# Operator stage of a graph network kernel: the bias by matrix-vector steps between the blocks of the powers, edge weights by an indirect load, node degrees in the main part, one wait for each input at the head

## The chip, the cores and the metric

The kernel runs on one core of one Trainium2 chip. Its time is the device time of one execution in microseconds, as the median of several runs. The core has TensorE (PE, matmuls), VectorE (DVE), ScalarE (ACT), GpSimd (POOL) and SyncE (SP, which issues most loads and stores); each works through its own list of instructions in order, and semaphores tie them together.

## What is computed

Four layers of graph networks over x (16 x 512 x 128), each added to x and normalised. What matters here is the first one and what the later ones need from the adjacency and the edge list:

```python
def _L0_gnn_ref(x, adj_mx, alpha_train, w, d, fc_in_w, fc_in_b, vt):
    x0 = x
    h = jnp.einsum('bnd,ed->bne', x, fc_in_w) + fc_in_b
    alph = jax.nn.sigmoid(alpha_train)[:, None]
    w_eff = w * jnp.clip(d, 0.0, 1.0) @ w.T
    dt = 1 / 8
    for _ in range(8):
        ax = jnp.einsum('nm,bmd->bnd', adj_mx, h)
        h = h + dt * (alph * 0.5 * (ax - h) + h @ w_eff - h + x0)
    return h
# layer 2: deg = row sums + column sums - diagonal of (A + I); dinv = rsqrt(deg)
# layer 3: e = e + jnp.log(A0[src, dst] + EPS)[None, :, None]     (256 edges)
```

The eight steps are linear in h, so the kernel writes their result as a polynomial in L (512 x 512: a scaled adjacency with its diagonal) and R (128 x 128, from w_eff): it needs the first, second and third power of L, eight powers of R, nine matrices E of 128 x 128, and one bias over nodes and features that stands for fc_in_b.

## The kernel before

`phase_operators` (lines 85 to 550) makes these operators once, `phase_main` (from 632) runs layers 1 and 2, then come `phase_batchnorm` and `phase_attention`. Each phase is a block that all engines leave together, so the main part starts when the last engine of the operator stage is done. TensorE works on 8 banks of PSUM in the hand-written `order` (lines 162 to 164): `begin(name, needs)` (424) waits until VectorE has emptied the tile seven places back and those it needs, `done` reports the tile. A power of L is built in four tiles (`L2T0` to `L2T3`, `L3T0` to `L3T3`; `l_power`, 448), each of 4 x 3 matmuls of 128x128 by 128x512 (`product`, lines 63 to 67: high by high, high by low, low by high; so the records stand at lines 65 to 67). ScalarE copies each tile's high part (244) and VectorE subtracts for the low part (`split` and `low_part`, line 72).

At the head (lines 184 to 232) SP loads w, the whole adjacency A in one piece, the edge lists and then x; ScalarE's queue loads alpha, d, the bias and fc_in_w, and its sigmoid (232) waits for the first three of them. VectorE makes L from A in four row blocks (279, 281), ScalarE rounds each (236), VectorE takes the low parts (285), and TensorE transposes L when all of it is there (438 to 443).

The bias goes by Horner's rule: U holds (0, 1, row sums of L) and is multiplied by L once (`UT`, 476); V holds combinations of the powers of R with the bias (498); `B2` and `B01T` (504, 510) multiply the two, and two steps `T` and `S` with the third power of L (`bias_horner`, 457) follow behind the last power, each turned back by four transposes (468).

The edge weights A[src, dst] are found with matmuls: sorted one-hot rows `Gs` of the sources are multiplied with all of A (`ROWS0`, `ROWS1`, 538), masked with the targets' `Gd` (411) and summed (`LG`, 548); ScalarE takes the logarithm (251). The sorting permutation (`perm`, 336) gives the sorted ends (`PERM`, 529; `SMALL`, 522), which SP writes to memory (197). The degrees come from row sums (355), column sums on TensorE (517), and the diagonal (357, 359); GpSimd takes the root (220), and `DROW` (544) makes a row of them that SP writes out (200).

VectorE also builds the matrices E: 9 starts (347) and 36 updates (369) from the powers of R. In the main part the prologue (`prologue`, line 821) mixes set-up tiles (`set_tiles`: transposes of A and the LSTM weights) with the first samples; `row_sum_diagonal`, at line 1614, scales the identity by the row sums.

## Time and profile before

| what | us |
|---|---|
| median of three runs (1060.51 to 1065.15) | 1063.21 |
| the profiled execution | 1063.46 |
| its span in the profile | 1061.5 |
| PE busy | 947.9 (89%) |
| DVE busy | 678.0 (64%) |
| ACT busy | 540.3 (51%) |
| POOL busy | 300.6 (28%) |

The profile is one execution. Times are counted from the start of its span. A row of a time line names the start, the duration, the engine and line, the operation, the tile written and the tiles read, shapes, and how many like instructions were merged into it; in brackets stands the idle time before it and who ended it. Matmuls overlap, so the distance between starts says more of their cost than the duration. An fp32 matmul leaves two records, one with fp32r operands one.

### The profile page before, as it was taken

The page shows a single profiled execution, that of the slowest core. Times are in us where ns is not written, and L with a number is a line of the kernel's source. Part 1 is how long each engine was busy: PE and PEld are TensorE (multiplying, and loading weights), DVE is VectorE, ACT ScalarE, POOL GpSimd, SP SyncE. Part 2 cuts the span into 40 slices and gives each one's busy share as a digit, 9 for nine tenths or more (in the row PEclk, how much of TensorE's full clock was granted, in tenths as well). Part 3 has the DMA queues.
Part 4 walks back from the last instruction along what each step waited for, and adds up shares of the span by engine and source line. Part 5 has one row for each costly group of instructions (what it writes and reads, how often), then busy time and mean ns, then how long its engine had stood idle before and what let it go on. Part 6 is the DMA issues. An engine that isn't in the chain of part 4 may idle for free. (4 is left out here: it accounts for less than half of the span.)

```text
span 1061.5 us, 14487 instructions
## 1 busy us (share of the span) xinstructions
PE 947.9 (89%) x5168; PEld 810.5 (76%) x5168; DVE 678.0 (64%) x1653; ACT 540.3 (51%) x1114; POOL 300.6 (28%) x279
## 2 busy tenths in 40 slices
PE   3989998889998999999899999989989987768984
PEld 2677997778998788899788998878778974355763
DVE  4843434434565744775674675568887875779897
ACT  2023233365554555564555545356667747466644
POOL 0001121223231312333222332232342230045643
PEclk9989999999999999999999999999999998889987
DMA  8003001000101010001001010301010000000014
GB/s 213 1 1 78 21 40 60 21 20 1 41 1 41 1 40 20 6 35 41 1 2 39 20 41 1 106 12 40 21 41 20 2 0 1 1 1 1 1 40 119
DMA packets 33881, 31.61 MB, mean 30 GB/s; under 512 B 8338, under 2 KB 27922, under 8 KB 33812
## 3 DMA queue, kind: packets, MB, share of 16 engines
q1 hardware_dynamic: 32852, 30.64, 9.3%
q8 instruction: 41, 0.67, 0.3%
q14 instruction: 28, 0.23, 0.1%
q10 hardware_dynamic: 960, 0.07, 0.1%
HBM read 22.83 MB, written 7.87 MB: 29 GB/s over the span
## 5 line engine op out<-in xcount | busy, mean ns | idle before, releaser
L1306 ACT ACTIVATE gates<-psum,gbias 128x256 f32<-128x256 f32 (+2 forms) x312 | 158.2, 565 | 56.5 <-PE psum L67 52.8
L65 PE MATMUL psum<-LS,WI 128*128 128x256 f32 (+2 forms) x312 | 105.5, 338 | 14.0 <-ACT gates L1306 10.2
L72 POOL TENSOR_TENSOR LS<-A,LS 128x512 fp32r<-128x512 f32 (+2 forms) x44 | 48.8, 1109 | 202.1 <-ACT LS L1291 202.1
L66 PE MATMUL psum<-LS,WI 128*128 128x256 f32 (+2 forms) x312 | 104.2, 334 | 0.0
L67 PE MATMUL psum<-LS,WI 128*128 128x256 f32 (+2 forms) x312 | 104.2, 334 | 0.0
L72 POOL TENSOR_TENSOR LS<-Hodd,LS 128x512 fp32r<-128x512 f32 (+2 forms) x44 | 48.6, 1106 | 160.2 <-ACT LS L1291 160.2
L65 PEld LDWEIGHTS psum<-LS,WI 128*128 128x128 f32 x312 | 60.4, 194 | 25.6 <-POOL LS L72 10.3
L72 DVE TENSOR_TENSOR yl<-psum,yh 128x512 fp32r<-128x512 f32 x58 | 39.7, 689 | 57.2 <-ACT yh L1248 41.4
L65 PE MATMUL psum<-B2h,LT2h 128*128 128x256 f32 x256 | 72.8, 284 | 1.1 <-DVE X L1414 1.0
L1313 ACT ACTIVATE tc<-cell 128x512 f32<-128x512 f32 (+2 forms) x88 | 45.2, 514 | 55.7 <-DVE cell L1594 39.9
L67 PE MATMUL psum<-B2h,LT2l 128*128 128x256 f32 x256 | 72.4, 283 | 0.0
L66 PE MATMUL psum<-B2l,LT2h 128*128 128x256 f32 x256 | 72.4, 283 | 0.0
L65 PE MATMUL psum<-Eh,yh 128*128 128x384 f32 x168 | 58.5, 348 | 12.0 <-DVE yl L72 12.0
L66 PEld LDWEIGHTS psum<-LS,WI 128*128 128x128 f32 x312 | 60.5, 194 | 5.1
L67 PEld LDWEIGHTS psum<-LS,WI 128*128 128x128 f32 x312 | 60.6, 194 | 4.2
L72 POOL TENSOR_TENSOR XSl<-X,XSh 128x512 fp32r<-128x512 f32 x32 | 42.4, 1329 | 69.0 <-ACT XSh L1243 68.7
L65 PE MATMUL psum<-LS,WH 128*128 128x256 f32 (+2 forms) x192 | 60.1, 313 | 0.0
L66 PE MATMUL psum<-LS,WH 128*128 128x256 f32 (+2 forms) x192 | 59.8, 312 | 0.0
L67 PE MATMUL psum<-LS,WH 128*128 128x256 f32 (+2 forms) x192 | 59.8, 312 | 0.0
L67 PE MATMUL psum<-Eh,yl 128*128 128x384 f32 x168 | 57.7, 344 | 0.0
L66 PE MATMUL psum<-El,yh 128*128 128x384 f32 x168 | 57.6, 343 | 0.0
L566 DVE BATCH_NORM_STATS2 nstats<-X 128x6 f32<-128x128 f32 x256 | 54.1, 277 | 0.4
(387 smaller groups left out, 2714.6 us busy)
## 6 DMA issues: line engine op xcount, KB each, us to landing
WI<-lstm_weights SPq DMA_DIRECT2D x14, 512.0 KB, 3.5
WH<-lstm_weights SPq DMA_DIRECT2D x11, 512.0 KB, 4.5
X<-in_x SPq DMA_DIRECT2D x16, 256.0 KB, 4.8
out<-X SPq DMA_DIRECT2D x16, 256.0 KB, 2.3
lstm_weights<-WI SPq DMA_DIRECT2D x4, 512.0 KB, 2.6
lstm_weights<-WH SPq DMA_DIRECT2D x3, 512.0 KB, 2.6
A<-in_adj SPq DMA_DIRECT2D x1, 1024.0 KB, 5.9
z_A<-in_adj SPq DMA_DIRECT2D x1, 1024.0 KB, 5.4
```

Source lines behind the costliest of these rows:

```text
L65: pe.matmul(out, lhs[0], rhs[0], start=start, stop=False)
L66: pe.matmul(out, lhs[0], rhs[1], start=False, stop=False)
L67: return pe.matmul(out, lhs[1], rhs[0], start=False, stop=stop)
L72: return eng.tensor_tensor(out, full, high.bitcast(F32), ALU.subtract)
L566: return dve.bn_stats(self.stats[:, bass.ds(self.sh.C * n + c, 1), :], self.sh.X[:, c, bass.ds(n, 1), :])
L1306: act.activation(gates[:, gate, 0:n], sh.psum[:, gate, 0:n], ACT.Tanh if gate == G else ACT.Sigmoid, bias=gbias[:, p_ - 1, gate:gate + 1]) ...
L1313: act.activation(tcs[:, 0:n], cell[:, s % 2, 0:n], ACT.Tanh).then_inc(S["tanh_done"], 1)
```

## The change

The bias is built from matrix-vector steps. Four groups `UA` to `UD` hold pairs of vectors (ones, and L applied to them again and again) in high and low parts, 4 columns in all; `UA` multiplies by L, `UB` to `UD` by the second power, each in 8 wide matmuls that stand between the blocks of the powers. After each of the first three, four transposes (`TA`, `TB`, `TC`) bring the vectors back, and VectorE adds high and low and splits again. `BIAS` multiplies the four groups by V in 16 small products at the very end. The Horner steps, `B2`, `B01T` and `UT` are gone.

The edge weights are loaded by GpSimd with two indirect loads of 128 elements each, at addresses that VectorE computes from src and dst; they are spread to 16 columns and multiplied by the permutation (`LG`). The row gathering with A and its masks are gone, and `PERM` and `SMALL` stand earlier.

Column sums, diagonal, root and the row of the degrees move to the main part's prologue: the column sums come from VectorE over the transposed tiles of A, the row is one more set-up tile `deg`, and its write stands in SP's list there.

At the head A comes in four pieces with a semaphore each, alpha, d and the bias have one each, the broadcast edge lists are loaded behind the first four pieces of x; the transposes go row block by row block; the low parts of L go to GpSimd; the first block of the second power waits piece by piece. wTd is made after L. VectorE's 36 updates of E are cut into pieces between its other work, and ScalarE's copy of E comes after `L3T2` instead of `L2T3`.

```diff
-        order = ["wT", "R", *(f"LT{j}" for j in range(C)), "R2", "UT", "L2T0", "R34", "L2T1", "R58", "L2T2", "FR03",
-                 "L2T3", "FR47", "FR8V", "L3T0", "B2", "L3T1", "B01T0", "B01T1", "L3T2", "L3T3", "SMALL", "T", "PERM", "T'",
-                 "ROWS0", "ROWS1", "S", "DROW", "S'", "LG"]
+        a_in = [sem(f"a_in_{c}") for c in range(C)]
+
+
+        order = ["wT", *(f"LT{j}" for j in range(C)), "R", "L2T0", "R2", "L2T1", "UA", "R34", "L2T2", "R58", "L2T3",
+                 "PERM", "SMALL", "TA", "FR03", "FR47", "FR8", "UB", "L3T0", "TB", "V", "UC", "L3T1", "TC", "LG", "UD",
+                 "L3T2", "L3T3", "BIAS"]
         at = {n: i for i, n in enumerate(order)}
-        his = [n for n in order if n[:2] in ("LT", "L2", "L3", "B2", "T'")]
+        his = [n for n in order if n[:2] in ("LT", "L2", "L3") and n != "LG"]
...
+        def rows_of(j):
+
+            if j == 0:
+                return 0, (2,)
+            if j == 1:
+                return 0, (0,)
+            g, r = divmod(j - 1, 2)
+            return g, (r, r + 2)
...
-            sp.dma_start(sh.A[:, :, :], d["adj"].rearrange("(c p) m -> p c m", p=P)).then_inc(S["a_in"], 16)
+            for c in range(C):
+                sp.dma_start(sh.A[:, c, :], d["adj"][c * P:(c + 1) * P, :]).then_inc(a_in[c], 16)
...
+                if q == 0:
+                    for k, name in enumerate(("src", "dst")):
+                        sp.dma_start(ir[:, k, :], d[f"L3_gnn_{name}"].rearrange("(o e) -> o e", o=1)
+                                     .broadcast_to([P, NE])).then_inc(S["ir_in"], 16)
...
-            sp.wait_ge(S["dve_tile"], at["DROW"] + 1)
-            sp.dma_start(sh.degrees, drow[0:1, :]).then_inc(S["ss_done"], 16)
-            sp.wait_ge(S["ss_done"], 32)
+            sp.wait_ge(S["ss_done"], 16)
...
+            for c in range(C):
+                pool.wait_ge(S["lh_done"], c + 1)
+                low_part(pool, Ll[:, c, :], L[:, c, :], Lh[:, c, :]).then_inc(S["ll_done"], 1)
+            for k, value in enumerate(sh.const_values):
+                pool.memset(sh.const[:, k, :], value).then_inc(S["memsets"], 1)
+            pool.wait_ge(S["at_done"], 1)
+            table = d["adj"].rearrange("s (t o) -> (s t) o", o=1)
+            for k in range(K):
+                pool.indirect_dma_start(weight[:, k:k + 1], None, table,
+                                        bass.IndirectOffsetOnAxis(at_edge[:, k:k + 1], 0)).then_inc(S["weight_in"], 16)
+            pool.wait_ge(S["weight_in"], 16 * K)
...
-            act.wait_ge(S["small_in"], 48)
+            act.wait_ge(S["al_in"], 16)
...
-                if name == f"L2T{C - 1}":
+                if name == "L3T2":
...
-            act.wait_ge(S["pe_tile"], at["LG"] + 1)
+            act.wait_ge(S["dve_tile"], at["LG"] + 1)
...
+            def vectors_split():
+
+                link(dve.tensor_copy(U[:, :, 0:2], pair[:, :, :]))
+                low_part(dve, U[:, :, 2:4], pair[:, :, :], U[:, :, 0:2]).then_inc(S["u_done"], 1)
+
+            def vectors_out(g):
+                copy(f"U{groups[g]}", UT[:, g, :], bank(f"U{groups[g]}")[0:W, :])
+
+            def vectors_turned(g):
+                name = f"T{groups[g]}"
+                tile(name)
+                ins = dve.tensor_copy(turned[:, :, :], bank(name)[:, 0:C * W].rearrange("p (c r) -> p c r", r=W))
+                ins.then_inc(S["dve_tile"], 1)
+                dve.wait_ge(S["dve_tile"], at[name] + 1)
+                if g == 0:
+                    dve.tensor_copy(pair[:, :, 0:1], turned[:, :, 0:1])
+                    link(dve.tensor_tensor(pair[:, :, 1:2], turned[:, :, 1:2], turned[:, :, 3:4], ALU.add))
+                else:
+                    link(dve.tensor_tensor(pair[:, :, :], turned[:, :, 0:2], turned[:, :, 2:4], ALU.add))
+                vectors_split()
...
+            dve.wait_ge(S["dc_in"], 16)
+            link(dve.tensor_scalar(dclip[:, :], dcol[:, :], 0.0, 1.0, ALU.max, ALU.min))
+            dve.tensor_scalar(wTd[:, :], wT[:, :], dclip[:, 0:1], DT, ALU.mult, ALU.mult)\
+                .then_inc(S["dve_tile"], 1)
+            row_sums(0, 2)
+            copy("R", RP[:, 1, :], bank("R")[:, 0:D])
+            link(row_sums(2, C))
+            link(dve.tensor_tensor(pair[:, :, 1], sh.rs[:, :], kappa[:, :], ALU.mult))
+            dve.wait_ge(S["memsets"], 5)
+            link(dve.tensor_tensor(pair[:, :, 1], pair[:, :, 1], ldiag[:, :], ALU.add))
+            vectors_split()
+            split("L2T0")
+            dve.wait_ge(S["ic_in"], 32)
+            link(dve.tensor_copy(icf[:, :, :], icol[:, :, :]))
+            link(dve.scalar_tensor_tensor(at_edgef[:, :], icf[:, 0, :], float(N), icf[:, 1, :], ALU.mult, ALU.add))
+            dve.tensor_copy(at_edge[:, :], at_edgef[:, :]).then_inc(S["at_done"], 1)
+            dve.wait_ge(S["ir_in"], 32)
+            split("L2T1")
+            tile("UA")
+            dve.tensor_scalar(UT[:, 0, :], bank("UA")[0:W, :], sh.ident[0:W, 2:3], None, ALU.add)\
+                .then_inc(S["dve_tile"], 1)
+            copy("R34", RP[:, 3:5, :], bank("R34")[:, 0:2 * D].rearrange("p (k d) -> p k d", d=D))
+            split("L2T2")
+            copy("R58", RP[:, 5:9, :], bank("R58").rearrange("p (k d) -> p k d", d=D))
+            dve.wait_ge(S["bc_in"], 16)
+            for j in range(NCO):
+                for r in rows_of(j)[1]:
+                    ins = dve.tensor_scalar(bsel[:, j, r:r + 1], bcol[:, 0:1], binom(N_STEPS, j), None, ALU.mult)
+            ins.then_inc(S["bsel_done"], 1)
+            split("L2T3")
+            copy("PERM", ss[:, :, :], bank("PERM").rearrange("p (j e) -> p j e", j=2))
+            copy("SMALL", sh.sc[:, :], bank("SMALL")[:, 0:K])
+            vectors_turned(0)
...
+            start_e("FR03", 0, 4)
+            start_e("FR47", 4, 4)
+            start_e("FR8", 8, 1)
+            vectors_out(1)
+            vectors_turned(1)
+            copy("V", V[:, :, :], bank("V")[0:W, :].rearrange("p (g d) -> p g d", d=D))
+            dve.wait_ge(S["weight_in"], 16 * K)
+            for k in range(K):
+                ins = dve.tensor_scalar(weightb[:, k, :], ones[:, 0:R], weight[:, k:k + 1], None, ALU.mult)
+            ins.then_inc(S["spread_done"], 1)
+            dve.wait_ge(S["dve_tile"], at["FR8"] + 1)
+            link(forcing(0))
+            vectors_out(2)
+            split("L3T1")
+            vectors_turned(2)
+            copy("LG", weights[:, :], bank("LG")[0:R, 0:NE])
+            for i in (1, 2, 3):
+                link(forcing(i))
+            vectors_out(3)
+            for i in (4, 5, 6):
+                link(forcing(i))
+            forcing(7).then_inc(S["e_done"], 1)
+            split("L3T2")
...
+            copy("BIAS", sh.bias0[:, :, :], bank("BIAS").rearrange("p (c d) -> p c d", d=D))
...
+                begin(f"L{r}T{j}", [] if r == 2 else [f"L{r - 1}T{C - 1}"])
+                    if r == 2 and j == 0:
+                        pe.wait_ge(S["ll_done"], k + 1)
+                        pe.wait_ge(S["dve_tile"], at[f"LT{k}"] + 1)
...
+            def vectors(g):
+
+                name = f"U{groups[g]}"
+                begin(name, [] if g == 0 else [f"L2T{C - 1}"])
+                pe.wait_ge(S["u_done"], g + 1)
+                high, low = sh.LT[0 if g == 0 else 1]
+                for k in range(C):
+                    pe.matmul(bank(name)[0:W, :], U[:, k, :], high[:, k, :], start=(k == 0), stop=False)
+                for k in range(C):
+                    ins = pe.matmul(bank(name)[0:2, :], U[:, k, 0:2], low[:, k, :], start=False, stop=(k == C - 1))
+                done(ins)
+            def turn(g):
+                name = f"T{groups[g]}"
+                begin(name, [f"U{groups[g]}"])
                 for c in range(C):
...
+            l_power(2, 0)
+            r_power("R2", 1, 1, "R")
+            l_power(2, 1)
+            vectors(0)
+            r_power("R34", 2, 2, "R2")
+            l_power(2, 2)
+            r_power("R58", 4, 4, "R34")
+            l_power(2, 3)
+            begin("PERM")
+            begin("SMALL")
+            for q in range(K):
+                for k in range(K):
+                    ins = pe.matmul(bank("SMALL")[:, q:q + 1], perm[:, k, q * P:(q + 1) * P], icf[:, 0, k:k + 1],
+                                    start=(k == 0), stop=(k == K - 1))
+            done(ins)
+            turn(0)
+            pe.wait_ge(S["fc_in"], 16)
+            forced("FR03", 0, 4)
+            forced("FR47", 4, 4)
+            forced("FR8", 8, 1)
+            vectors(1)
+            l_power(3, 0)
+            turn(1)
+            begin("V")
+            pe.wait_ge(S["bsel_done"], 1)
+            sizes = {}
+            for j in range(NCO):
+                sizes.setdefault(rows_of(j)[0], []).append(j)
+            for g, members in sizes.items():
+                for j in members:
+                    ins = pe.matmul(bank("V")[0:W, g * D:(g + 1) * D], bsel[:, j, :], RP[:, N_STEPS - j, :],
+                                    start=(j == members[0]), stop=(j == members[-1]))
+            done(ins)
+            vectors(2)
+            l_power(3, 1)
+            turn(2)
+            begin("LG")
+            pe.wait_ge(S["spread_done"], 1)
+            for k in range(K):
+                ins = pe.matmul(bank("LG")[0:R, 0:NE], weightb[:, k, :], perm[:, k, :], start=(k == 0),
+                                stop=(k == K - 1))
+            done(ins)
+            vectors(3)
+            l_power(3, 2)
+            l_power(3, 3)
+            begin("BIAS", ["UD", "V"])
+                cols = slice(c * P, (c + 1) * P)
+                for g in range(NG):
+                    ins = pe.matmul(bank("BIAS")[:, cols], UT[:, g, cols], V[:, g, :], start=(g == 0),
+                                    stop=(g == NG - 1))
...
-        set_tiles = [("A", j) for j in range(C)] + [("rs", 0), ("WI", 2), ("WI", 3), ("WH", 1), ("WH", 2), ("WI", 0),
+        set_tiles = [("A", j) for j in range(C)] + [("rs", 0), ("WI", 2), ("WI", 3), ("WH", 1), ("WH", 2), ("deg", 0), ("WI", 0),
                                                     ("WI", 1), ("WH", 0)]
...
+                     [next(late)], [("own", 2)], giant("t", 0, 0), taps(0, 3), [("own", 3)],
...
+                if kind == "deg":
+                    sp.wait_ge(S["set_free"], n + 1)
+                    sp.dma_start(sh.degrees, degree_row).then_inc(S["deg_out"], 16)
...
+                elif kind == "deg":
+                    dve.wait_ge(S["set_mm"], n + 1)
+                    dve.tensor_copy(degree_row, bank_like(n, "A")[0:1, :]).then_inc(S["set_free"], 1)
                 else:
-                    dve.wait_ge(S["set_hi"], n + 1 - (n > C))
+                    dve.wait_ge(S["set_hi"], turned_before(n) + 1)
+                    if kind == "A":
+                        dve.reduce_sum(cs[:, j:j + 1], bank_like(n, kind), AX.X)
...
+                if q == 0 and k == 0:
+                    dve.wait_ge(S["deg_out"], 16)
...
+            def degrees():
+                dve.wait_ge(S["set_mm"], FIRST_SUMS + 1)
+                for c in range(C):
+                    ins = dve.tensor_tensor(diag[:, c, :], sh.A[:, c, c * P:(c + 1) * P], sh.ident[:, :], ALU.mult)
+                link(ins)
+                dve.tensor_tensor(deg[:, :], rs[:, :], cs[:, :], ALU.add)
+                link(dve.reduce_sum(dsum[:, :], diag, AX.X))
+                dve.scalar_tensor_tensor(deg[:, :], deg[:, :], 1.0, dsum[:, :], ALU.add, ALU.subtract)\
+                    .then_inc(S["deg_done"], 1)
+
+            def root_diagonal():
+                dve.wait_ge(S["dinv_done"], 1)
+                for c in range(C):
+                    ins = dve.tensor_scalar(diag[:, c, :], sh.ident[:, :], sh.dinv[:, c:c + 1], None, ALU.mult)
+                ins.then_inc(S["roots_done"], 1)
...
+            def degree_roots():
+                pool.wait_ge(S["deg_done"], 1)
+                pool.tensor_tensor(sh.dinv[:, :], deg[:, :], sh.const[:, sh.ROOT, 0:C], ALU.pow)\
+                    .then_inc(S["dinv_done"], 1)
...
```

## Rows read from the trace of the kernel before

**Rows 1.** The page, busy time: engine, us, share of the span, instructions.
```profile
PE 947.9 (89%) x5168; PEld 810.5 (76%) x5168; DVE 678.0 (64%) x1653; ACT 540.3 (51%) x1114; POOL 300.6 (28%) x279
```
**Rows 2.** Windows of the operator stage: stretch, its length, each engine's busy time, clock, DMA.
```profile
26.18:59.95 33.77, 32.83 (x138) 23.92 (x137) 26.81 (x93) 5.50 (x9) 0.00 (x0) 0.95 0.00 1
59.95:89.36 29.41, 25.93 (x124) 20.91 (x122) 10.87 (x26) 2.97 (x5) 1.02 (x1) 0.88 0.00 1
89.36:130.00 40.64, 40.64 (x235) 36.94 (x236) 18.07 (x44) 14.24 (x37) 7.74 (x6) 1.00 0.28 65
...
53.20:56.30 3.10, 3.10 (x8) 2.38 (x8) 1.63 (x7) 1.33 (x2) 0.00 (x0) 0.50 0.00 0
...
64.00:70.00 6.00, 6.00 (x18) 4.95 (x18) 0.23 (x2) 0.00 (x0) 1.02 (x1) 0.50 0.00 0
```
**Rows 3.** Time line at the end of the stage, VectorE, ScalarE and TensorE.
```profile
86.80 0.68 DVE L297 COPY bias<-psum 128x512 f32<-128x512 f32 x1
88.60 0.46 ACT L251 ACTIVATE lg<-psum,tiny 16x256 f32<-16x256 f32 x1 [13.99 <-PE psum L548]
...
89.36 0.63 PE L1047 MATMUL psum<-ident,X 128*128 128x128 f32 x4 [0.80 <-PEq L99]
```
**Rows 4.** DMA issues of the head: tile, issuing queue, size, us to landing.
```profile
A<-in_adj SPq DMA_DIRECT2D x1, 1024.0 KB, 5.9
...
alpha<-in_L_gnn_alpha_train ACTq DMA_DIRECT2D x1, 2.0 KB, 2.4
...
bcol<-in_L_gnn_fc_in_b ACTq DMA_DIRECT2D x1, 0.5 KB, 7.1
```
**Rows 5.** Time line of the head: ScalarE (first two, last), VectorE.
```profile
2.76 1.28 ACT L232 ACT_TABLE_LOAD   x1 [2.76 <-issue]
8.88 0.20 ACT L232 ACTIVATE gate<-alpha 128x4 f32<-128x4 f32 x1 [4.84 <-DMA bcol<-in_L_gnn_fc_in_b]
...
10.11 0.48 DVE L279 TENSOR_SCALAR L<-A,kappa 128x512 f32<-128x512 f32 x1
...
13.25 2.49 DVE L72 TENSOR_TENSOR Ll<-L,Lh 128x512 fp32r<-128x512 f32 x4
...
29.18 0.60 ACT L244 ACTIVATE LT1h<-psum 128x512 fp32r<-128x512 f32 x1 [11.48 <-PE psum L67]
```
**Rows 6.** GpSimd's time line at 110 us, and line 1614's durations, min/median/max in ns.
```profile
110.47 1.29 POOL L1699 TENSOR_TENSOR X<-X,bias 128x512 f32<-128x512 f32 x1 [4.82 <-DVE X L1414]
...
L1614 DVE TENSOR_SCALAR cell<-ident,rs x4: 164/274/1314, 110.4 to 112.0; 128x128 f32<-128x128 f32 x4
```
**Rows 7.** Time line of TensorE: transposes, first of UT's twelve, first of L2T0's, R34.
```profile
13.39 3.68 PE L441 MATMUL psum<-ident,L 128*128 128x128 f32 x16 [2.34 <-DVE L L281]
...
21.38 0.59 PE L65 MATMUL psum<-LT0h,Uh 128*3 128x512 f32 x1 [3.88 <-DVE LT0l L72]
...
26.18 0.39 PE L65 MATMUL psum<-LT0h,Lh 128*128 128x512 f32 x1
...
28.98 0.59 PE L446 MATMUL psum<-RP 128*128 128x256 f32 x2
```
**Rows 8.** Time line of TensorE: the small and the fp32 products.
```profile
46.73 1.15 PE L504 MATMUL psum<-V,UT 3*128 3x128 f32 x8 [0.94 <-DVE V L363]
...
50.79 1.98 PE L510 MATMUL psum<-UT,V 3*128 3x512 f32 x4
...
59.95 3.66 PE L517 MATMUL psum<-ones,A 128*128 128x1 f32 x32
...
85.13 1.02 PE L544 MATMUL psum<-dblock,ones 128*128 128x512 f32 x2
86.08 0.66 PE L468 MATMUL psum<-ident,bt 128*128 128x128 f32 x4
```
**Rows 9.** Time line of VectorE: the 36 updates of E, and E's low part.
```profile
46.71 8.22 DVE L369 SCALAR_TENSOR_TENSOR Ef<-RP,Ef 128x128 f32<-128x128 f32 x36
...
57.26 1.35 DVE L72 TENSOR_TENSOR El<-Ef,Eh 128x1152 fp32r<-128x1152 f32 x1
```

More of the change, by code:

```diff
@@ new lines, in row_sums @@
+            def row_sums(c0, c1):
+                for c in range(c0, c1):
+                    ins = dve.reduce_sum(sh.rs[:, c:c + 1], sh.A[:, c, :], AX.X)
+                return ins
+            dve.wait_ge(S["idn"], 1)
+            dve.tensor_copy(RP[:, 0, :], sh.ident[:, :])
+            tile("wT")
+            link(dve.tensor_copy(wT[:, :], bank("wT")[:, 0:D]))
+            dve.wait_ge(S["gate_done"], 1)
+            link(dve.tensor_scalar(kappa[:, :], gate[:, :], 0.5 * DT, None, ALU.mult))
@@ L527, in _ @@
+            begin("R", ["wT"])
+            done(pe.matmul(bank("R")[:, 0:D], wTd[:, :], wT[:, :], start=True, stop=True))
+            l_power(2, 0)
[7 more added lines that the diff above has]
+            begin("PERM")
+            pe.wait_ge(S["perm_done"], 1)
             for j in (0, 1):
@@ L542, in _ @@
-            begin("DROW")
-            pe.wait_ge(S["diag_done"], 1)
-            done(pe.matmul(bank("DROW"), ones[:, :], dblock[:, :, :], start=True, stop=True))
-            turned("S", 1)
-            begin("LG", ["ROWS1"])
+            begin("SMALL")
[3 more added lines that the diff above has]
+                                    start=(k == 0), stop=(k == K - 1))
@@ L690, in phase_main @@
         rs = sh.rs
+        degree_row = cell[0:1, 1, :]
         norm = sh.norm
```

308 lines of the change are left out of this document (68 added, 240 removed).

## The prediction

> **What bounds the kernel now.** I read the page first: PE is busy 89% of the span [rows 1], so time can be won only where PE waits or where its work is taken away. Then I looked at the stretches around the changed code. The operator stage runs from 0 to 89.36 us, where the first instruction of the main part starts; every block ends in a barrier, so the question is when that instruction can start [rows 2, 3]. The stage has three pieces. Up to 26.18 the head waits for inputs: PE is mostly idle, and when it works, UT's twelve 512-column matmuls take 4.80 us, 21.38 to 26.18, of which the last two already went at the later 0.23: the other ten stood (4.80-0.47)/10 = 0.43 apart [rows 7] (the clock column reads 1.00 here [rows 2]; the spacing tells the half pace). From 26.18 to 59.95 PE is full with the powers of L. From 59.95 to 89.36, 29.4 us, PE does sums over the adjacency, two Horner steps for the bias, and the edge one-hots. That tail is serial and partly at half clock (0.50 in 64 to 70) [rows 2]. Every microsecond taken off this stage moves all of the rest, since nothing later waits for an input that starts early: the loads are out by 26 us [rows 2].
>
> **The head.** ScalarE's gate waits for alpha, dcol and bcol together: alpha lands at 0.73+2.4 = 3.1, bcol at 1.79+7.1 = 8.9, and the gate runs at 8.88 [rows 4, 5]. With its own semaphore the gate waits only for the table load, 2.76+1.28 = 4.04. VectorE then has kappa and ldiag by about 5.0. A's four pieces replace one load that landed at 1.18+5.9 = 7.1 [rows 4]; I take the last piece at 7.1 to 7.5 and the earlier ones about 1 us apart. Scaling one block of rows costs (13.25-10.11)/4 = 0.79 us [rows 5], so without a collision all L stands at 8.2, against 13.3 before.
>
> There is a collision. The low parts of L go from VectorE (four in 2.49) to GpSimd, which takes 1.29 us for a 128x512 operation of two inputs [rows 6], and the first starts at about 6.5 while VectorE is still scaling. The trace has this pair once: during a GpSimd addition of the same shape, 1.29 us (110.47), one of VectorE's four scalings grew from 0.27 to 1.31 us [rows 6]. That is one holding the other off, not sharing. The Trainium skill (SBUF — State Buffer, "SBUF: two separate sides") says that the two engines take a common port pair as an exclusive lock, held for the whole instruction, when VectorE reads two SBUF inputs or is in a two-port mode; by it L's last two blocks each wait for one GpSimd operation, as that row does. I take two such waits, 2.6 us (bounds 0 and three waits, 3.9), on the path: L at 10.8. Behind that the last four of sixteen transposes take 0.9 at half pace (3.68/4) [rows 7], ending at 11.7, but VectorE has more to do: dclip and wTd 0.5, half a wait more on wTd 0.6, two row sums and the first split at 0.62 each, 1.9 [rows 5]. The first L-square block starts at 13.8, not at 26.18.
>
> **PE's work from there.** That block is 12 matmuls at half pace: 12 x 0.43 = 5.1 us, to 18.9. The vector step UT, 12 matmuls between 21.38 and 26.18 and 4.8 us long at half pace, is gone from in front of it [rows 7]. All that follows in PE's order, at full clock: seven more blocks of 26.18 to 28.98 = 2.80: 19.6 [rows 7]; four vector steps of 8 wide matmuls at 2.80/12 = 0.233: 7.5 (they weigh as much with 4 stationary columns as with 128, since UT's 12, with 3 columns, also took the 0.43 of the half pace); three turns of four transposes, 0.6 each by L468 (0.66 with its tail): 1.8; fp32 products: three of 512 columns at 0.95 (L544 at 85.13, the next product at 86.08), one of 256 at 0.4, two of 128 at 0.3: 3.9; V, nine products of 128 columns at the 0.23 of L517's sixteen small ones (3.66), 2.1; SMALL, four of them, 0.9; PERM, four of 256 columns at half of 0.95, 1.9; LG, two of these, 0.9; and BIAS, 16 products with 4 rows: L504 has four with 3 rows in 1.15, so 16 x 0.29 = 4.6 [rows 8]
>
> Sum 43.2, to 62.1. Of the old tail (29.4) the column sums, two Horner steps, eight transposes, the gathering of rows and the degree row are gone.
>
> **Waits in that order.** PE needs VectorE's answers, so I ran VectorE's list beside it. Its largest load, the 36 Ef updates in 8.22 us [rows 9], is now cut into pieces behind the vector steps. PE's one wait comes out at UD: after L3T1 come ScalarE's copy (0.6 [rows 5]), the split (0.6) and the turned sum and split (0.8), 2.2 us in all, of which TC and LG cover 1.4: 0.8. PERM's mask is ready some 0.3 us before PE wants it. If the splits were each 0.5 us later, UB, UC and UD would wait 1.5 us more together. At the end VectorE has the Ef updates done 4 us ahead of BIAS's end; then ScalarE's Eh, the 1.35 of El, and a split [rows 9] fit under BIAS with 1 us over. ScalarE's table load and the logarithm (0.46) also lie under BIAS, where before they ended the stage at 89.06 [rows 3].
>
> The indirect load: indices are ready at about 21, VectorE asks for the weights at about 44. No row shows such a load. The nearest are strided loads of 4-byte elements, 2.4 to 7.1 us from issue to landing (alpha, bcol) [rows 4]; two in series end by 26 to 36, so within these bounds the cost is nothing, covered by PE's blocks; uncovered it is theirs whole, rival (c). Edge rows are written out to memory earlier than before, no one waits for them. SP's queue: three more A issues put X's loads a microsecond or two later, still over 30 us ahead of need; the broadcast index rows sit behind X's first four pieces (about 13 us, wanted at 19).
>
> **Clock.** The clock fell to 0.50 at 53.2, right after PE had spent 2 us on products with three rows (L510 at 50.79), and again at 64, after L517's 3.5 us of one-column products [rows 2, 8]. BIAS is 4.6 us of four-row products followed by 1 us of copy and barrier. I expect a fall inside BIAS or right after. Half clock for half of BIAS would cost 2.3; I take 1.0, since the fall may come behind it (0 to 3.5). And 3 to 5 us of half clock at the start of the main part, where PE is busy without a gap [rows 2], cost 1.6 (0 to 2.6).
>
> Stage end: 62.1 + 0.8 + 1.0 = 63.9; copy of the bias 0.7 and barrier 0.3 (before: the copy from 86.80, ScalarE to 89.06, PE at 89.36) [rows 3]: 64.9. Saved: 24.5.
>
> **The main part** takes what is moved there. PE: one product like L544, 0.95. VectorE: four column sums (2.5), the degree chain (2.0), the root diagonal (0.9), a one-row copy (0.7): 6.1 us on an engine that is busy 18.07 of 40.64 us there, with PE waiting for it seldom; 0.5 (0 to 3). GpSimd's root (1.0) and its wait for the degrees stand before a split of x that is asked for much later; if it isn't, 1 us. SP's degree write stands between the weight spills; the first cell step waits for it, some 40 us later. With the clock's 1.6: 3.1 lost.
>
> Net: 24.5 - 3.1 = 21.4. The profiled execution is 1063.46 us (span 1061.5), within 0.3 of the median of the three runs; 1063.46 - 21.4 = 1042.1, rounded to 1042.
>
> **Rivals.** (a) No collision and no fall of the clock: 3.2, 1.0 and 1.6 less, 1036, down to 1032 if BIAS runs faster. For it: the port row is one case, and the operations may interleave well. (b) VectorE becomes the bound of the stage: each of the four vector steps has a chain PE, copy, turn, sum, split, PE, and each link in it takes 0.6 or more; three steps late by 2 us, Ef late by 2 and the 3 of the main part give +8 to +14: 1050 to 1056. Against it: VectorE was idle a good part of 26 to 60 (26.8 of 33.8 busy, with 4.8 of that moved away) [rows 2]. (c) Slower than before: the indirect load. VectorE waits for the weights in front of Ef, so in the last third of the stage everything queues behind them. The first 23 us after the indices are hidden; each further one is paid whole. From 23+22 = 45 us the gain is gone, at 50 the kernel is 5 us slower, 1069. Nothing in the trace comes near, but no such load is in it. (d) The finer waits and the order don't shorten anything, since some wait that I have not seen (a bank of the ring, a semaphore count) holds PE to the old pace: about 1060 to 1066.
>
> **Chances.** Forecast, 1034 to 1049: 0.72. (a) below 1034: 0.10. (b), 1049 to 1058: 0.13. (d) 0.02, (c) 0.03. The range, from 8 us below the forecast to 7 above, takes in the collision's and the clock's bounds and the small stalls: 1034 to 1049. About 0.5% (5 us) is what a measurement of this kernel tells from no change: faster 0.95, same 0.02, slower 0.03.
>
> **What would show it.** The first main transposes (L1047 of before) at 62 to 67 us; the gate at about 4; L's last scaling at 10 to 12 with one VectorE row over 1 us beside a GpSimd subtraction; the first L-square block at 12 to 15; PE without a wait over 1 us from there to BIAS; clock 0.50 around the change of stage; the weights landed before 36. The forecast is wrong if PE waits for VectorE in several places between the blocks, if BIAS's products cost much more than 0.29, or if the main part grows by more than 5 us.

## The result and the profile after

The changed kernel takes 1038.02 us in the median of four runs (1037.67 to 1042.06), the kernel before 1063.51 in the same comparison: ratio 0.9774, interval 0.975 to 0.9797. Forecast were 1042, with 1034 to 1049 as the range. The profiled execution took 1037.67 us, its span is 1035.6; against 1061.5 before that is 25.9 us less. First, from the page of the changed kernel, the span, the busy time of the engines and the new queue of the indirect loads.

```profile
span 1035.6 us, 14415 instructions
PE 932.7 (90%) x5120; PEld 798.0 (77%) x5120; DVE 676.9 (65%) x1662; ACT 540.0 (52%) x1112; POOL 308.2 (30%) x284
...
q0 software_dynamic: 64, 0.00, 0.0%
```

PE's busy time fell by 15.2 us [rows 1], 10.7 us less than the span: the rest is waiting that went away. The time lines of the changed kernel at the turn from the operator stage to the main part, PE, then VectorE (columns as in the rows of before):

```profile
56.31 3.83 PE L530 MATMUL psum<-V,UT 4*128 4x128 f32 x32
61.19 1.02 PE L1045 MATMUL psum<-ident,X 128*128 128x128 f32 x4 [1.05 <-PEq L99]
```
```profile
57.15 1.36 DVE L72 TENSOR_TENSOR El<-Ef,Eh 128x1152 fp32r<-128x1152 f32 x1 [0.63 <-ACT Eh L247]
58.43 0.68 DVE L72 TENSOR_TENSOR LT2l<-psum,LT2h 128x512 fp32r<-128x512 f32 x1
60.18 0.69 DVE L273 COPY bias<-psum 128x512 f32<-128x512 f32 x1 [1.07 <-PE psum L530]
```

The first main transpose runs at 61.19, before at 89.36 [rows 3]: the stage is 28.2 us shorter. The main part is 2.3 us longer (1035.6-61.19 = 974.4 against 1061.5-89.36 = 972.1). 28.2 less 2.3 is the 25.9. The 2.3 comes from one pair of profiles and is less sure than the 28.2: in three runs below with the main part of the kernel before, the span behind the first main transpose is 967.0 to 972.4 us long, and in six with that of the changed kernel, again begun at half clock, 970.9 to 974.8. The second fence shows El and the last split done at 59.1, under BIAS, which ends at 60.14. VectorE then waits 1.07 us for BIAS: PE sets the end of the stage, with one microsecond to spare.

VectorE's time line over the head of the changed kernel, and GpSimd's beside it:

```profile
4.86 0.49 DVE L310 TENSOR_SCALAR L<-A,kappa 128x512 f32<-128x512 f32 x1
5.38 0.35 DVE L312 SCALAR_TENSOR_TENSOR L<-ident,ldiag,L 128x128 f32<-128x128 f32 x1
...
6.56 1.47 DVE L310 TENSOR_SCALAR L<-A,kappa 128x512 f32<-128x512 f32 x1
8.07 1.23 DVE L312 SCALAR_TENSOR_TENSOR L<-ident,ldiag,L 128x128 f32<-128x128 f32 x1
...
10.18 1.21 DVE L316 TENSOR_SCALAR wTd<-wT,dclip 128x128 f32<-128x128 f32 x1
```
```profile
6.48 2.67 POOL L72 TENSOR_TENSOR Ll<-L,Lh 128x512 fp32r<-128x512 f32 x2 [4.30 <-ACT Lh L240]
10.04 2.50 POOL L72 TENSOR_TENSOR Ll<-L,Lh 128x512 fp32r<-128x512 f32 x2 [0.89 <-ACT Lh L240]
```

Three of VectorE's rows are 0.9 to 1.0 us longer than their twins: 1.47 against 0.49, 1.23 against 0.35, and wTd with 1.21 against the 0.29 of the kernel before. Each lies beside one of GpSimd's subtractions, and L is done at 10.08.

PE's time line in the changed kernel at the first block of the second power (13.33), the first product behind it (17.82), the vector step UA, a turn, and UD:

```profile
13.33 0.76 PE L65 MATMUL psum<-LT0h,Lh 128*128 128x512 f32 x1 [1.08 <-DVE LT0l L72]
...
17.82 0.38 PE L425 MATMUL psum<-RP 128*128 128x128 f32 x2
...
20.84 1.09 PE L446 MATMUL psum<-LT0h,U 128*4 128x512 f32 x4
...
46.50 0.41 PE L455 MATMUL psum<-ident,UT 4*128 4x4 f32 x4
...
48.76 1.09 PE L446 MATMUL psum<-LT1h,U 128*4 128x512 f32 x4 [0.89 <-DVE U L72]
```

Between 17 us and the barrier at 61 only the last of these has a wait, at UD: 0.89 us.

PE in windows of the changed kernel around the turn (stretch, its length, PE busy with instructions, granted clock, share of the DMA engines, GB/s), and the transposes of A in the main part:

```profile
58.00:60.00 2.00, 2.00 (x20) 1.00 0.00 0
60.00:62.00 2.00, 0.95 (x6) 0.82 0.00 0
62.00:64.00 2.00, 2.00 (x12) 0.50 0.31 85
64.00:66.00 2.00, 2.00 (x12) 0.83 0.59 110
```
```profile
62.01 3.23 PE L1033 MATMUL psum<-ident,A 128*128 128x128 f32 x16
```

The clock falls not inside BIAS but behind it, and the main part starts at 1.2 GHz: the sixteen transposes of A take 3.23 us.

### The profile page after: what moved, and what is told of

Same layout as the page of the kernel before. It is cut to its first block and busy times, and to the rows that moved or that the text cites. A ratio compares the mean times of both kernels' runs of the same rounds, so it can differ in the third digit from the quotient of the medians.

```text
span 1035.6 us, 14415 instructions
## 1 busy us (share of the span) xinstructions
PE 932.7 (90%) x5120; PEld 798.0 (77%) x5120; DVE 676.9 (65%) x1662; ACT 540.0 (52%) x1112; POOL 308.2 (30%) x284
## 5 line engine op out<-in xcount | busy, mean ns | idle before, releaser
L1304 ACT ACTIVATE gates<-psum,gbias 128x256 f32<-128x256 f32 (+2 forms) x312 | 158.3, 565 | 56.3 <-PE psum L67 52.7
```

Of the source, the lines that this page charges most:

```text
L1304: act.activation(gates[:, gate, 0:n], sh.psum[:, gate, 0:n], ACT.Tanh if gate == G else ACT.Sigmoid, bias=gbias[:, p_ - 1, gate:gate + 1]) ...
```

## The experiments

The theory after the result: the stage is a list of PE work with one small wait; the head pays for VectorE and GpSimd holding each other off; the four-row products of BIAS bring the fall of the clock; the indirect load is hidden. The place of the first main transpose (61.19) is read from one profile and tells more finely than the medians, which scatter by some microseconds: in the comparisons of the experiments the kernel before itself took 1062.04 and 1064.59 us in the median, and 1059.25 in the one run beside the single runs. So each ratio is to the kernel before of its own comparison, and times of different comparisons are not subtracted here to a microsecond. The place has a scatter of its own: with the same head, the first block of the second power starts between 13.27 and 13.84, as the first piece of A lands earlier or later.

**Full rows for BIAS.** The products are the same in number and columns; the vectors and V lie in 128 rows, 124 of them zero.

```diff
-        V = sb("V", [W, NG, D])
-        UT = sb("UT", [W, NG, N])
+        V = sb("V", [P, NG, D])
+        UT = sb("UT", [P, NG, N])
...
+            pool.memset(UT[:, :, :], 0.0).then_inc(S["memsets"], 1)
+            pool.memset(V[:, :, :], 0.0).then_inc(S["memsets"], 1)
```

> The changed kernel, but UT and V have 128 rows, 124 of them zero, so that the 16 products of BIAS use 128 rows instead of 4; the result is unchanged. If the clock falls at 60 us because PE's last 3.8 us before the main part were products with four rows, the granted clock stays 1.00 through the change of stage, the first wide matmul of the main part comes 2.1 us after its first transpose (as before the change) instead of 3.8, and the kernel is 1.7 us faster than the changed one (about 1036.3, ratio to before 0.975). Rival: the gap of 1 us at the barrier, or the small products whatever their rows (128 columns each), bring the clock down: then 0.50 again from 60.5 to 65.5 and no gain. BIAS itself should take its 3.8 us in both.

It measured 1035.12 us (1034.74 to 1035.99), ratio 0.9754 (0.9732 to 0.9777). PE's time line and windows of this kernel:

```profile
56.52 3.73 PE L532 MATMUL psum<-V,UT 128*128 128x128 f32 x32
61.31 0.63 PE L1047 MATMUL psum<-ident,X 128*128 128x128 f32 x4 [1.06 <-PEq L99]
61.77 1.91 PE L1035 MATMUL psum<-ident,A 128*128 128x128 f32 x16
```
```profile
60.00:61.00 1.00, 0.25 (x3) 1.00 0.00 0
62.00:63.00 1.00, 1.00 (x12) 1.00 0.31 93
64.00:65.00 1.00, 1.00 (x6) 1.00 0.39 48
```

The products cost the same (3.73 against 3.83), the same pause of 1.06 us follows, and the clock stays at 1.00. Nothing else differs at this place, so with the few rows of BIAS this pause lets the clock fall, and with full rows it does not. The other runs agree: in all seven profiles in which the four-row BIAS stands last, the first wide matmul of the main part comes 2.8 to 3.2 us after the first transpose of A, in the two with full rows 1.7. Few rows are not the only thing that a fall can follow, though; the run without the bias below shows another. The first wide matmul of the main part comes 2.13 us after the first transpose (63.44), as it did before the change, against 3.80 in the changed kernel: 1.7 us. The Trainium skill (TensorE: Matmul & The Clock Gate, "Part 1: The HAM clock gate (the "warmup" mystery)") lets the clock follow how busy PE has been; PE was busy without a gap in both kernels here, so by the records' busy time alone the two should not differ.

**Low parts of L only after wTd.** GpSimd waits until VectorE is through with its scalings.

```diff
+            pool.wait_ge(S["dve_tile"], at["wT"] + 1)
             for c in range(C):
                 pool.wait_ge(S["lh_done"], c + 1)
```

> The changed kernel, but GpSimd begins with the low parts of L only when VectorE has made wTd, so nothing of it lies beside the scaling of L. If GpSimd and VectorE hold each other off, the three stretched rows of VectorE (scaling 1.47, diagonal 1.23, wTd 1.21 us against 0.49, 0.35, 0.29) go back to their short lengths, L is done 1.9 us earlier (8.2 instead of 10.1), wTd 2.8 us earlier, and the first L-square block starts at 10.6 to 11.3 instead of 13.33; GpSimd's 1.25 us each then pace that block's four parts, which match PE's 1.3 at half clock. The kernel is 2.0 to 2.7 us faster than the changed one, 1035.5. Rival: the stretching comes from A's pieces landing or from memory traffic of the loads; then the rows stay long and the block starts later than 13.3, since the low parts come later: 0 to 2 us slower than the changed one.

1035.87 us (1035.01 to 1036.54), ratio 0.9761 (0.9738 to 0.9783). VectorE's rows, GpSimd's, and PE's first block and first main transpose in this kernel:

```profile
6.74 0.49 DVE L311 TENSOR_SCALAR L<-A,kappa 128x512 f32<-128x512 f32 x1
...
8.62 0.29 DVE L317 TENSOR_SCALAR wTd<-wT,dclip 128x128 f32<-128x128 f32 x1
```
```profile
8.99 4.98 POOL L72 TENSOR_TENSOR Ll<-L,Lh 128x512 fp32r<-128x512 f32 x4 [6.81 <-DVE wTd L317]
```
```profile
10.84 0.77 PE L65 MATMUL psum<-LT0h,Lh 128*128 128x512 f32 x1 [0.72 <-DVE LT0l L72]
...
58.62 1.06 PE L1046 MATMUL psum<-ident,X 128*128 128x128 f32 x4 [1.05 <-PEq L99]
```

No row is stretched, the block starts 2.5 us earlier and the main part at 58.62, 2.57 earlier. The four pieces of A land beside VectorE's scalings here too, so the loads did not stretch them, as the rival had it. The four subtractions start 2.5 us later and nobody misses them. The rule of the Trainium skill that the prediction drew on (SBUF — State Buffer, "SBUF: two separate sides") holds here, also for the 128x128 operation of two inputs.

**Low parts on VectorE as before.** The same four subtractions move back behind wTd.

```diff
-            for c in range(C):
-                pool.wait_ge(S["lh_done"], c + 1)
-                low_part(pool, Ll[:, c, :], L[:, c, :], Lh[:, c, :]).then_inc(S["ll_done"], 1)
...
+            for c in range(C):
+                dve.wait_ge(S["lh_done"], c + 1)
+                low_part(dve, Ll[:, c, :], L[:, c, :], Lh[:, c, :]).then_inc(S["ll_done"], 1)
```

> The changed kernel with this one part undone: the low parts of L on VectorE again (four of 0.62 us), behind wTd. Theory: the 2.5 us of work that return are about what the collisions cost (0.98+0.88+0.92 = 2.8), so the first L-square block starts at 12.9 to 13.4 (13.33 in the changed kernel) and the time is the same within 0.5 us, 1038. Rival, that the move to GpSimd was worth its 2.5 us: the block at 15 to 16 and the kernel 2 us slower.

1037.70 us (1035.74 to 1042.22), ratio 0.9783 (0.9747 to 0.9819). L is ready at 8.6 and the block starts at 13.34, main at 61.11: by its places the same as the changed kernel. The 2.5 us of work that VectorE gave away came back as 2.8 us of being held off.

**Both mends together**, with the row sums of L put behind the splits:

```diff
+            pool.wait_ge(S["dve_tile"], at["wT"] + 1)
...
-            row_sums(0, 2)
             copy("R", RP[:, 1, :], bank("R")[:, 0:D])
...
-            link(row_sums(2, C))
+            link(row_sums(0, C))
```

> The changed kernel with three things together: UT and V padded with zeros to 128 rows (clock stays up: 1.7 us, as measured alone), GpSimd's low parts behind wTd (first L-square block at 10.84 instead of 13.33: 2.5 us, as measured alone), and the first two row sums moved behind the splits of L's transposes (1.2 us less in front of the block; GpSimd's first low part is then the last input, so 0.3 to 0.8 of it). If the gains are in series they add: 4.5 to 5, main part at 57.9 to 58.4, clock 1.00 there, 1033.2 (ratio to before 0.972 to 0.973). Rival: an earlier block meets the half clock longer, or VectorE's list (Ef, E's low part) comes to bound the end of the stage, since it has 1 us over there; then 3 to 4.

1033.64 us (1029.23 to 1034.12), ratio 0.9712 (0.9692 to 0.9732), the fastest version of this study. PE in this kernel at its first block and at the turn:

```profile
10.58 0.77 PE L65 MATMUL psum<-LT0h,Lh 128*128 128x512 f32 x1 [0.44 <-DVE LT0l L72]
...
58.07 0.63 PE L1047 MATMUL psum<-ident,X 128*128 128x128 f32 x4 [1.05 <-PEq L99]
```

3.1 us come from the earlier main part and 1.7 from the clock, 4.8 together, which are the 4.5 to 5 expected. The medians differ by 4.4, from different comparisons. Moving the row sums was worth little: the block comes 0.3 earlier than with the wait alone.

**The indirect loads four and eight times**, each pair waited for:

```diff
-            for k in range(K):
-                pool.indirect_dma_start(weight[:, k:k + 1], None, table,
+            for again in range(8):
+                for k in range(K):
+                    pool.indirect_dma_start(weight[:, k:k + 1], None, table,
...
+                pool.wait_ge(S["weight_in"], 16 * K * (again + 1))
```

> The changed kernel with the pair of indirect loads done four times in series, each pair waited for. The pair takes from 20.3 to 22.9 to issue and an unseen time to land; by this run's second pair it can be read. I expect 4 to 5 us for a pair, the fourth pair landed at 37 to 40, before VectorE asks for the weights at 42.5: main part at 61.2, kernel unchanged. Rival: a pair takes over 7 us, and what passes 42.5 is paid whole.

> The same with eight pairs. At 4 to 5 us each the last lands at 52 to 60, 10 to 18 us after VectorE asks for it at 42.5, and with VectorE held in front of the first updates of Ef nearly all of that is paid: main part at 71 to 79 and the kernel 9 to 17 us slower than the changed one. This measures the price and the point of decision of the rival on the slower side. Rival: VectorE catches up in its idle time under PE's blocks, and less than half of the lateness is paid.

Four pairs: 1037.22 us in a single run, main at 61.18, nothing moved. Eight pairs: 1047.86, also a single run, main at 71.78. GpSimd's time line with four pairs (first two), VectorE's and PE's with eight:

```profile
20.22 1.37 POOL L225 DMA_INDIRECT weight<-in_adj,at_edge  x1 [7.41 <-DVE at_edge L334]
21.89 0.94 POOL L225 DMA_INDIRECT weight<-in_adj,at_edge  x1 [0.30 <-issue]
24.51 0.94 POOL L225 DMA_INDIRECT weight<-in_adj,at_edge  x1 [1.67 <-DMA weight<-in_adj,at_edge]
```
```profile
52.49 0.37 DVE L393 TENSOR_SCALAR weightb<-ones,weight 128x16 f32<-128x16 f32 x2 [9.82 <-DMA weight<-in_adj,at_edge]
```
```profile
71.78 1.09 PE L1047 MATMUL psum<-ident,X 128*128 128x128 f32 x4 [1.06 <-PEq L99]
```

A pair takes 4.3 us the first time and 3.8 to 4.0 after, once 5.1 among the eight. VectorE wants the weights at 42.46 in the changed kernel and one pair is there at 24.5: 18 us of cover. Once it is used up VectorE comes 10.0 us late and the main part 10.6: what exceeds the cover is paid whole. The reading for this is that the Ef updates, El and the splits queue behind that wait. Rival (c) had the mechanism and its price right, and only the size of one load wrong.

**The head alone, in the kernel before**: pieces of A, a semaphore for each small load, transposes by row block, wTd behind L; the low parts stay on VectorE, the bias, the edges and the degrees as they were.

```diff
-            sp.dma_start(sh.A[:, :, :], d["adj"].rearrange("(c p) m -> p c m", p=P)).then_inc(S["a_in"], 16)
+            for c in range(C):
+                sp.dma_start(sh.A[:, c, :], d["adj"][c * P:(c + 1) * P, :]).then_inc(a_in[c], 16)
...
-            act.wait_ge(S["small_in"], 48)
+            act.wait_ge(S["al_in"], 16)
```

> The kernel before, with the finer head alone: A in four pieces, alpha, d and bias with a wait each, transposes row block by row block, wTd behind L, index rows behind x; low parts stay on VectorE, and the bias, the edge weights and the degrees stay as before. Theory: L is done at 8.1 instead of 13.3, and as every later step of the stage is in series behind it, 4.5 to 5.5 us come through to the end: first transpose of the main part at 84 to 85 (89.36 before), kernel 1058.3, ratio 0.995. The head's share of the 28.2 us is then a fifth. Rival: PE is at half clock there and the low parts and row sums of VectorE bound the head, so that only 2 to 3 us come through.

1059.32 us (1057.34 to 1061.36), ratio 0.9973 (0.9958 to 0.9988). The first block starts at 22.07, 4.1 us earlier than before, but the main part at 86.97, only 2.4 earlier. The missing 1.7 us stand in the gathering of rows. Its row in the kernel before, then the same row and PE's windows in this kernel:

```profile
75.36 7.14 PE L538 MATMUL psum<-Gs,A 128*128 128x256 f32 x32 [2.68 <-DVE Gs L399]
```
```profile
71.27 8.83 PE L541 MATMUL psum<-Gs,A 128*128 128x256 f32 x32 [2.68 <-DVE Gs L401]
```
```profile
70.00:74.00 4.00, 2.73 (x9) 0.81 0.00 0
74.00:78.00 4.00, 4.00 (x16) 0.76 0.00 0
```

The same stretch in the kernel before:

```profile
74.00:76.00 2.00, 0.64 (x3) 1.00 0.00 0
76.00:78.00 2.00, 2.00 (x11) 1.00 0.00 0
```

The wait ahead of the gathering is the same 2.68 us, but it takes 8.83 us: part of it runs at 1.2 GHz here, with a mean granted clock of 0.81 and 0.76. In both kernels the clock had fallen once ahead of this work, behind the column sums (0.50 in 64 to 70 before [rows 2], 0.50 in 60 to 64 here); in this kernel it falls a second time behind the wait, where it stayed at 1.00 before. The wait is equally long and the work around it the same in both, so why it fell in one of them stays open. I had expected main at 84 to 85: of a gain at the head 1.7 us did not arrive, since a stretch of half clock came up in the tail.

**The bias left out**, in the kernel before and in the changed one: no vectors, no products for it, bias0 set to zero.

```diff
-            copy("BIAS", sh.bias0[:, :, :], bank("BIAS").rearrange("p (c d) -> p c d", d=D))
+            dve.memset(sh.bias0[:, :, :], 0.0)
```

> The kernel before without its bias: UT, V, B2, B01T, both Horner steps and their transposes are left out, and the bias is zero. By the rows of before this takes from PE 4.8 (UT), 2.1 (V), 1.15+0.94 (B2 and its wait), 2.0 (B01T), 5.2 and 3.0 (the steps), 1.3 (transposes), 20.5 in all, less what comes up as waits for VectorE's one-hots and E: the first transpose of the main part at 70 to 73 instead of 89.36, kernel 1044 to 1047. Rival: the tail is set by the chain of the edge weights (PERM, masks, rows, sum, logarithm) and not by the bias, and only about 10 us go.

> The changed kernel without its bias: UA to UD, the turns, V and BIAS are left out, and the bias is zero. By its rows PE loses 4 x 1.86, 1.0 of turns, 2.1 of V, 0.9 of waiting, 3.8 of BIAS = 15.2. VectorE's list then bounds the end (Ef, E's low part, the last split), so 12 to 15 come out: the main part at 46.5 to 49 instead of 61.19. With the run of the old kernel without bias this parts the 28.2 us: the bias alone accounts for (89.36 - old without) - (61.19 - new without), about 17.5 - 13.5 = 4, and the rest, head, edges and degrees, for about 24. Rival: the new bias is nearly free (under 7 us), since its products fill waits, and the bias is the largest part of the gain.

Old kernel without its bias: 1041.69 us in a single run, main at 67.27, so the old bias costs 22.1 us of the stage. New kernel without its bias: 1026.52, also a single run, main at 51.45, so the new one costs 9.7. Both expectations missed, the old one too low and the new one too high, and with them the share of 4 us: the rival, by which the bias is the largest part of the gain, was right. In the old kernel one of the two stretches of half clock, 53.2 to 56.3 [rows 2], goes with the bias and counts in the 22.1. PE of the old and of the new kernel without bias, with a window behind the second, then VectorE of the new:

```profile
67.27 0.63 PE L1000 MATMUL psum<-ident,X 128*128 128x128 f32 x4 [0.80 <-PEq L99]
```
```profile
51.45 1.08 PE L1003 MATMUL psum<-ident,X 128*128 128x128 f32 x4 [5.43 <-PEq L99]
52.33 3.62 PE L991 MATMUL psum<-ident,A 128*128 128x128 f32 x16
```
```profile
53.00:55.00 2.00, 2.00 (x11) 0.50 0.35 64
```
```profile
40.94 6.47 DVE L366 SCALAR_TENSOR_TENSOR Ef<-RP,Ef 128x128 f32<-128x128 f32 x28
...
48.65 1.36 DVE L72 TENSOR_TENSOR El<-Ef,Eh 128x1152 fp32r<-128x1152 f32 x1 [0.63 <-ACT Eh L247]
```

PE's work for the new bias adds up to some 14 us (four vector steps 7.5, three turns 1.0, V 2.1, BIAS 3.8), but without it PE stands 5.43 us at the end and waits for VectorE's Ef, El and splits: the bias work lies partly over a list of VectorE's that would be there anyway. The difference, 22.1-9.7 = 12.4 us, is the bias's share.

The clock is at half here too when the main part starts (0.50 in 53 to 55, the sixteen transposes of A take 3.62 us), though PE's last work was a full block of the third power with all 128 rows in use: here the fall follows a wait of 5.43 us. The 1.06 us of the barrier did not do that in the kernel with full rows in BIAS.

**The edge weights left out**, in the kernel before (no row gathering, masks, sum) and in the changed one (no indirect load, no `LG`); the logarithm is a constant.

```diff
-            act.activation(sh.lg[:, :], weights[:, :], ACT.Ln, bias=tiny[0:R, 0:1])
...
+            dve.memset(sh.lg[:, :], -2.0)
```

> The kernel before without its edge weights: the one-hots, the gathering of rows, masks, the sum and the logarithm are left out and the logarithms are -2; PERM, SMALL and everything of bias and degrees stay. By the rows of before PE goes from the turn T' at 72.1 over ScalarE's and VectorE's split to the second step at 74.1, which takes 3.0, then the degree row and the last turn: first main transpose at 79.5 to 81 instead of 89.36, 8.5 to 10 us less. Rival: the clock goes down in the shorter tail and 2 us come back.

> The changed kernel without its edge weights: the indirect loads, their spreading, LG and the logarithm are left out, logarithms -2. LG's 0.95 us on PE covered part of the wait for UD's vectors, so the wait grows by nearly as much: first main transpose at 60.2 to 61.2 (61.19 in the changed kernel), 0 to 1 us less. With the old kernel without edges this gives the edges' share of the 28.2 us: 8 to 10. Rival: the loads or the spreading cost more than their rows show (port with VectorE's updates), and 2 us or more go.

Old kernel: 1049.27 us in a single run, main at 80.34, so the edges cost 9.0 there. New kernel: 1034.59, also a single run, main at 61.52, which is later than with them (61.19) and outside the 60.2 to 61.2 expected. Its first block started 0.5 us late (13.84 against 13.33), as VectorE's first scaling waited 0.74 us for A; with that taken off the edges cost 0.2. So their share is near 9 us, in one profile each.

**The degrees left out** of the changed kernel: no set-up tile for them, no sums, no root.

```diff
-        DEG = set_tiles.index(("deg", 0))
...
-                    if kind == "A":
-                        dve.reduce_sum(cs[:, j:j + 1], bank_like(n, kind), AX.X)
```

> The changed kernel with the degree work left out of the main part (column sums, diagonal, root, the product and row, its write; the inverse roots are 1 and the row is read from the adjacency, so the later layers compute something else). In the traces the prologue of the main part fell back 1.69 us by its first norm and another 0.48 by 191 us. If the 0.48 is the degree product (0.95 on PE, half of it beside a wait that was there anyway), it goes and the 1.69 stays: 0.5 us faster than the changed kernel, below what the timing separates but plain in the trace (the weight step L1475 133.35 us after the first main transpose instead of 133.83 or so). Rival: VectorE's 6 us cost more than the product, 2 us come back, and the first norm comes earlier too.

1037.99 us (1034.72 to 1042.23), ratio 0.977 (0.9742 to 0.9798): the time can't be told from that of the changed kernel. By places: the copy of `mixes` (L1475 in the changed kernel, row below) comes 106.33 us after the first main transpose there, and 105.87 without degrees (61.72 to 167.59): 0.46 us. The first normalisation (L1446 in the changed kernel) comes 55.08 and 55.07 us after it. VectorE in the changed kernel:

```profile
167.52 0.69 DVE L1475 COPY mixes<-psum 128x512 f32<-128x512 f32 x1 [2.03 <-PE psum L67]
```

The same copy stood at 193.51 before the change, so 25.99 us of gain are left there; an addition into B (L1423), earlier, stood at 128.66 and stands at 102.18, 26.48. The first 1.69 of the 28.17 go at the half-clock start, the next 0.49 for the degrees, and behind that hardly anything changes in this pair: 25.9 are left at the end of the span.

## Why the prediction was right, point by point

**The result** lies 4 us below the forecast and well inside the range. The stage saved 28.2 us instead of 24.5, the main part lost 2.3 instead of 3.1. The stage's 3.7 are the sum of misses that all went one way: the first block began 0.5 earlier and was 0.6 shorter, and PE's list behind it was 2.7 shorter. Little cancelled there, so the forecast hit by its terms, each of them a little too dear. The main part's 2.3 is a less sure number, as said above; by places in the trace 2.2 can be laid to causes.

**Head.** Gate at 4.07 (said 4.04). The collision cost 0.98+0.88+0.92 = 2.8 us over three rows, taken as 2.6 on L and 0.6 on wTd; L done at 10.08 (10.8), the block at 13.33 (13.8). Undone in one run, it gave back 2.5. The four pieces of A came as assumed, about 0.9 apart.

**PE's list.** The first block took 4.5 us, since the pace doubled before its end, not 5.1. From 17.82 to BIAS's end at 60.14 are 42.3 us where the prediction had 18.9 to 63.9, 45.0. The 2.7 too many are: 1.0 of clock inside BIAS, which did not fall there; 0.8 in BIAS itself, 3.83 instead of 4.6, as the price of a product with three rows was taken from four of them whose record has its own tail; and 0.8 in the three turns, 0.33 from a turn's start to the next (46.50 to 46.83) instead of 0.6. The 0.6 came from transposes (L468, 0.58 from its start to the next) with rows of 128x128, and a turn's row is 4x4. The other terms met within 0.1 in their sum, not one by one: the seven blocks took 19.9 and not 19.6, as a group of fp32 operands that follows one directly starts some 0.1 later, and the six fp32 products 3.4 and not 3.9. The mis-sized terms are thus short groups priced from groups of another shape or count. The distance between starts alone would not have mended them: four products with three rows stand 1.09 apart from the next group (46.73 to 47.82), which still gives 4.4 for sixteen, while the 0.23 at which the same prediction priced the nine products of V gives 3.7.

**Waits.** One at UD, 0.89, said 0.8. VectorE had 1 us over at the end, as said; rival (b) needed several late steps, and this one was the only one. The run without bias shows how near it is, though: whoever takes more than that 1 us off PE's list has VectorE as the bound of the stage's end.

**Clock.** A fall was forecast "inside BIAS or right after"; it came after. The start of the main part lost 1.7 us to it (said 1.6). The prediction laid it to the small products, from two stretches of before, one behind products with three rows and one behind products with one column; filling the rows up removed it. That the place was right owes something to luck: the rows of before showed what a fall had followed, but not what it needs, and the run with the finer head alone has a fall that nothing here explains. For rival (a), no collision and no fall, 1036 was worked out; the version that mends both, with the row sums moved as well, takes 1033.6.

**Degrees.** 0.5 us in the main part instead of 1.45 (0.95 on PE and 0.5 on VectorE). The rest of the engine work moved there found room.

**Indirect load.** Hidden, with 18 us of cover. The bounds for two loads were 5 to 15 us from strided loads; a pair took 4.3, a little under them.

**Where the 28.2 us come from.** Bias 12.4, edges 9; the other 6.8 are the finer waits at the head and the sums and products for the degrees that left the stage. The head alone gave 4.1 us at the first block and 2.4 at the end of the stage. These shares were not all measured in one setting and overlap, and stretches of half clock come and go with them, so how the 6.8 divide stays open.

## What to carry to other kernels

Lay the stage out as the list of the engine that is never idle, and run the second engine's list beside it: sum and one wait gave the end of a 61 us stage within 4 us. Price a short group from a row with the same shape and about the same count. Before work goes to an idle engine, look for what the busy engine does at that moment and whether a row of the trace shows the pair holding each other off; here the move alone was worth nothing, and with a wait of one line it was worth 2.5 us. And look at what PE does last before a change of stage: with few rows in use there, or after a wait of some microseconds, the next stage can start at half clock.

## What the runs showed of the hardware

Sixteen products with 4 rows are followed by a granted clock of 0.50, and the same sixteen with 128 rows, 124 of them zero, leave it at 1.00, for nearly the same time on PE (3.83 and 3.73 us), with a pause of 1.06 us behind either. A pause of 5.43 us behind wide matmuls with 128 rows is also followed by 0.50. An indirect load of 128 elements of 4 bytes holds GpSimd 0.94 us (the first 1.37) for its issue and is there about 2.6 us after it began; two in a row take 3.8 to 4.0 us, once 5.1. VectorE's 0.35 us operation of two inputs from SBUF takes 1.23 beside a GpSimd subtraction, as its scalings do.
